# A four-layer transformer on one core: a new order of work inside the linear-attention stage

## The chip, the cores and the metric

The kernel runs on one core of a Trainium2 chip (trn2). The metric is the device time of one execution in microseconds (us), lower is better. A core has a matrix engine (TensorE, PE in the profile; PEld is its weight load), a vector engine (VectorE, DVE), an activation engine (ScalarE, ACT), a general engine (GpSimd, POOL) and a queue for transfers (SyncE, SP). Each engine works through its own list of instructions in order; semaphores hold an instruction back until another engine has done something. Matrix products go to PSUM, eight banks of 512 fp32 columns on 128 partitions.

## The reference

Four layers of cross-attention and feed-forward on x of 16 x 128 x 256, all in fp32. The change lies in the attention of the second layer, a linear attention, and in the routing of the mixture of experts behind it, which the kernel computes beside it:

```
x = x + _L1_xattn_ref(_layernorm(x), ctx, ctx, mask, Wq, bq, Wk, bk, Wv, bv, Wqf, Wkf, Wo, bo)
x = x + _L1_ffn_ref(_layernorm(x), wg_router, ...)

def _L1_xattn_ref(query, key, value, attention_mask, ...):     # 16 heads of 16, 64 features
    q, k, v = heads(query, Wq, bq), heads(key, Wk, bk), heads(value, Wv, bv)
    q_prime = relu(einsum('bhnd,fd->bhnf', q, Wqf))
    k_prime = relu(einsum('bhnd,fd->bhnf', k, Wkf)) * attention_mask
    kv = einsum('bhnf,bhne->bhfe', k_prime, v)
    qkv = einsum('bhmf,bhfe->bhme', q_prime, kv)
    qk_sum = einsum('bhmf,bhf->bhm', q_prime, sum(k_prime))
    return (qkv / (qk_sum + 1e-08)) @ Wo.T + bo

# _L1_ffn_ref, its head: scores = softmax(x2d @ wg_router.T); top 6 of 32 experts;
# the place of each token in its expert = running count over all tokens; rows are sent there
```

## The kernel before

The stage is `linear_attention` (L1161). It works on 16 rows of the batch (128 tokens each, i = 0 to 15) in four groups of four (t = 0 to 3; j is the row in its group; g = t - 1 is the group before). Its work stands written out by hand, one list for each engine; nothing schedules it.

**A group's head.** PE projects the group's queries (Q0, Q1, into the two banks `proj`) and keys (K0, K1, into the two banks `wide`) with 512 columns each, and computes the query features in four rounds R00, R10, R01, R11 (`query_features`, L1263): each fills two banks, which ACT empties with a ReLU into `qf` (`move_features`, L1399) before they are used again. Before, R00, R10 and R11 go to `proj` and R01 to `wide`. Between them PE mixes and sums up the last rows of the group before (`mix_up(i-1)`, `sum_up(i-2)`, `sum_up(i-1)`). K1 goes to the bank in which the row before lies mixed, so it waits for that row's normalisation.

**A row's slot (j).** `key_features` (L1283, into `proj`; ACT masks them, `mask`), `turn_row` (L1269: a transpose of a normalised row of the next group, ACT moves it, `move_row`), `mix_up(i-1)`, `sum_up(i-2)`, `values(i+1)` (L1276), `pair_up(i)` (L1295, keys by values into `wide[0]`, ACT moves it). The values and the turned row share one bank, `value`, in its two halves; a matmul to one half waits until DVE or ACT has read the other.

**DVE** adds the bias to the values (`move_values`, L1463), normalises the mixed row (`normalize`, L1469: a reciprocal and a product), adds the summed row to x (`update`, L1477), and does the routing of the group before: `variance`, `shifts`, `scale` in the head, `find_slots` of the group before that in slot 0, `soften` and `choose` (L1045, the top 8 of 32) in slot 2, `pick` (L1062, counts) in slot 3.

**POOL** takes the roots for the norms (`root`), adds a bias to rows of x, and sends the rows of finished groups to the experts with indirect transfers (`scatter`, L1110, six to a row, each row waiting until the row before has landed). Its list is: root 0, biases, root 1, then four rows sent with a bias behind each, root 2, three rows sent, root 3, root 4. A group's rows can be sent once `find_slots` for the group is done. The next stage (experts) begins when all engines have ended this one, and opens with the other nine rows' transfers on POOL.

Lines that the timelines name: L1260 projections, L1266 query features, L1273 row turn, L1280 values, L1292 key features, L1301 pairs, L1312 mix, L1320 sum, L1014 and L1030 routing on PE; L1466 values' bias, L1471 and L1474 normalise, L1481 and L1483 update, L999 and L1003 shift and scale, L1049 to L1060 choose, L1067 to L1070 pick, L1095 to L1107 find slots on DVE; L994 root and L1116 scatter on POOL; L1421 on ACT hands DVE the divisor `z` of a mixed row.

## Time and profile before

| | us |
|---|---|
| median of 3 runs | 2010.26 (2008.82 to 2015.07) |
| the profiled execution | 2015.13 |
| its span in the trace | 2013.4 |
| linear-attention stage in it | about 698 to 893 |
| PE busy over the span | 1792.1 (89%) |
| DVE / ACT / POOL busy | 1264.2 / 1026.1 / 729.0 |
| granted TensorE clock, mean | 0.963 |

The chain of waits that the profile prints ends in the last stage, which the change does not touch, so it says nothing of this one. What binds here is read from the timelines of the engines: in each, a row is one instruction or a run of like ones, with its start, its busy time, the instruction, and in brackets the idle time ahead of it and what ended that.

### The profile page before, as it was taken

The page shows a single profiled execution, that of the slowest core. Times are in us where ns is not written, and L with a number is a line of the kernel's source. Part 1 is how long each engine was busy: PE and PEld are TensorE (multiplying, and loading weights), DVE is VectorE, ACT ScalarE, POOL GpSimd, SP SyncE. Part 2 cuts the span into 40 slices and gives each one's busy share as a digit, 9 for nine tenths or more (in the row PEclk, how much of TensorE's full clock was granted, in tenths as well). Part 3 has the DMA queues.
Part 4 walks back from the last instruction along what each step waited for, and adds up shares of the span by engine and source line. Part 5 has one row for each costly group of instructions (what it writes and reads, how often), then busy time and mean ns, then how long its engine had stood idle before and what let it go on. Part 6 is the DMA issues. An engine that isn't in the chain of part 4 may idle for free. (4 is left out here: it accounts for less than half of the span.)

```text
span 2013.4 us, 42500 instructions
## 1 busy us (share of the span) xinstructions
PE 1792.1 (89%) x12207; PEld 1211.7 (60%) x12216; DVE 1264.2 (63%) x4137; ACT 1026.1 (51%) x2698; POOL 729.0 (36%) x707
## 2 busy tenths in 40 slices
PE   7999999998999888859899999987997879999765
PEld 4677777775555556645566666663554555787533
DVE  5666666664777534565543344446997954787697
ACT  5555555554333344411344444435887942666586
POOL 3333333332000100557455555552320011998420
PEclk9999999999999999979999999998998889999888
DMA  9990000000000000135577777650001021222100
GB/s 311 304 274 0 0 0 0 0 0 1 0 0 0 1 1 1 70 135 176 142 164 161 164 162 171 117 123 1 2 2 66 1 70 41 43 54 58 36 22 22
DMA packets 145607, 145.55 MB, mean 72 GB/s; under 512 B 49376, under 2 KB 133568, under 8 KB 145344
## 3 DMA queue, kind: packets, MB, share of 16 engines
q1 hardware_dynamic: 122432, 113.81, 19.5%
q0 software_dynamic: 23040, 30.01, 8.5%
q8 instruction: 75, 1.23, 0.3%
q14 instruction: 60, 0.49, 0.1%
HBM read 137.12 MB, written 66.44 MB: 101 GB/s over the span
## 5 line engine op out<-in xcount | busy, mean ns | idle before, releaser
L1709 POOL DMA_INDIRECT expert_sums<-moe_rows_in,moe_to x128 | 198.2, 1549 | 159.2 <-DMA expert_sums<-moe_rows_in,moe_to 101.6
L1782 PE MATMUL moe_gate<-moe_places,moe_xt 128*128 x512 | 175.9, 466 | 4.2 <-issue 2.0
L1975 DVE COPY moe_ht_e<-moe_turned 128x256 f32<-128x256 f32 x128 | 54.3, 424 | 194.4 <-PE moe_turned L1790 194.4
L570 ACT ACTIVATE ga_prob<-ga_score,ga_neg_max 128x128 f32<-128x128 f32 x256 | 99.6, 390 | 125.7 <-DVE ga_neg_max L443 125.7
L2065 POOL TENSOR_TENSOR ln_rstd<-ln_var,half 128x4 f32<-128x4 f32 (+1 forms) x16 | 21.4, 1338 | 367.2 <-DVE ln_var L2061 367.2
L190 POOL TENSOR_TENSOR ga_q_inv<-ga_q_sum,half 128x4 f32<-128x4 f32 x64 | 64.4, 1007 | 224.4 <-DVE ga_q_sum L426 224.4
L3325 DVE CUSTOM_DVE_ANT_0 ctxt<-wa_score,early 128x128 f32<-128x128 f32 x512 | 110.8, 287 | 46.9 <-PE wa_score L3171 46.9
L3141 POOL TENSOR_TENSOR ctxt<-ctxt,wa_top 128x512 f32<-128x512 f32 x128 | 129.8, 1040 | 17.1 <-DVE wa_top L3325 17.1
L325 PE MATMUL ga_summed<-ga_wo,ga_out_t 128*128 128x256 f32 x512 | 121.2, 380 | 0.7 <-ACT ga_out_t L578 0.7
L1782 PEld LDWEIGHTS moe_gate<-moe_places,moe_xt 128*128 128x128 f32 x512 | 90.8, 190 | 48.6 <-issue 13.6
L249 PE MATMUL ga_proj<-early,ga_xt 128*128 128x512 f32 x252 | 119.8, 598 | 0.0
L1116 POOL DMA_INDIRECT slot_x<-early x96 | 98.6, 1027 | 54.1 <-issue 27.1
L439 DVE SCALAR_TENSOR_TENSOR ga_score<-ga_scored,ga_q_inv,ga_mask 128x128 f32<-128x128 f32 x256 | 72.2, 344 | 51.6 <-PE ga_scored L297 51.2
L325 PEld LDWEIGHTS ga_summed<-ga_wo,ga_out_t 128*128 128x128 f32 x512 | 92.3, 190 | 11.0 <-ACT ga_out_t L578 1.1
L1889 ACT ACTIVATE moe_act_e<-moe_gate 128x176 f32<-128x176 f32 x128 | 40.6, 317 | 101.6 <-PE moe_gate L1782 101.6
L3180 PE MATMUL wa_turned<-ident,ctxt 128*128 128x128 f32 x512 | 77.3, 286 | 11.3 <-POOL ctxt L3141 10.0
L3274 ACT ACTIVATE wa_pt<-wa_turned 128x512 f32<-128x512 f32 x128 | 73.1, 596 | 25.8 <-PE wa_turned L3180 23.3
L431 DVE COPY ga_qt<-ga_turned 128x512 f32<-128x512 f32 x63 | 43.4, 689 | 62.6 <-PE ga_turned L289 62.5
L297 PEld LDWEIGHTS ga_scored<-ga_kt,ga_qt 128*128 128x128 f32 x512 | 63.7, 192 | 23.6 <-DVE ga_qt L431 13.9
L556 ACT ACTIVATE ga_square<-ga_q_tok 128x128 f32<-128x128 f32 x256 | 75.0, 294 | 1.5 <-DVE ga_q_tok L394 1.4
L297 PE MATMUL ga_scored<-ga_kt,ga_qt 128*128 128x128 f32 x512 | 72.5, 285 | 0.9 <-DVE ga_qt L431 0.9
L1884 ACT ACTIVATE moe_xt<-moe_up 128x256 f32<-128x256 f32 x128 | 49.2, 384 | 47.0 <-PE moe_up L1771 36.5
(491 smaller groups left out, 4700.2 us busy)
## 6 DMA issues: line engine op xcount, KB each, us to landing
moe_places<-in_L_ffn_packed SPq DMA_DIRECT2D x128, 608.0 KB
slot_x<-zeros SPq DMA_DIRECT2D x24, 1076.0 KB, 14.8
moe_rows_in<-slot_x SPq DMA_DIRECT2D x128, 134.5 KB, 3.2
wa_v<-v_ctx SPq DMA_DIRECT2D x16, 180.0 KB, 3.2
early<-in_L_xattn_Wq SPq DMA_DIRECT2D x5, 512.0 KB, 7.8
x<-in_x SPq DMA_DIRECT2D x4, 512.0 KB, 9.6
ga_wo<-in_L_xattn_Wo SPq DMA_DIRECT2D x1, 2048.0 KB, 15.0
expert_sums<-zeros SPq DMA_DIRECT2D x2, 1024.0 KB, 7.9
```

The lines of the kernel that those rows point to most:

```text
L249: last = pe.matmul(proj[m % 2][:, :], lhs[:, c, :], weight[:, c, :], start=(c == 0), stop=(c == HC - 1))
L297: last = pe.matmul(scored[n % 2][:, h * P:(h + 1) * P], qt[:, n % 2, h * P:(h + 1) * P], kt[:, b % 2, g, :], start=True, stop=True)
L325: last = pe.matmul(summed[:, 0:H], out_t[:, h, :], w.wo[:, h, :], start=(h == 0), stop=(h == NH - 1))
L556: last = act.activation(square[:, h, :], q_tok[:, n % 2, h * D:(h + 1) * D], ACT.Square, accum_out=q_sum[:, n % 2, h:h + 1])
L570: last = act.activation(prob[:, n % 2, part], score[:, n % 2, part], ACT.Exp, bias=neg_max[:, n % 2, h:h + 1], accum_out=total[:, n % 2, h ...
L1116: pool.indirect_dma_start(out=self.mem.slot_x, out_offset=bass.IndirectOffsetOnAxis(ap=self.slot_to[:, t, k:k + 1], axis=0), in_=self.mem. ...
L1709: pool.indirect_dma_start(out=mem.sums[j % SUMS], out_offset=bass.IndirectOffsetOnAxis(ap=to[:, j:j + 1], axis=0), in_=y[:, j, :], in_offs ...
L1782: last = pe.matmul(both[j % 2][:, 0:2 * FE], xt[:, j % 2, c, :], packed[:, place, c * 2 * FE:(c + 1) * 2 * FE].rearrange("p a n -> p (a n) ...
L3141: pool.tensor_tensor(unit, unit, top[:, k % LOWS, :].unsqueeze(2).to_broadcast([P, QUAD, P]), ALU.subtract).then_inc(lowered.sem, 1)
L3180: last = pe.transpose(turned[k % 2][:, x * P:(x + 1) * P], low[:, k % LOWS, x, :], mem.ident[:, :])
L3274: act.activation(pt[:, k // 2, :, k % 2, :], turned[k % 2][:, :].rearrange("p (x m) -> p x m", x=QUAD), ACT.Exp).then_inc(pt_moved.sem, 1)
L3325: ins = dve.tensor_tensor_reduce(unit[:, x, :], score[k % QUAD][:, x * P:(x + 1) * P], w.table[:, k, x, :], 1.0, NEVER, ALU.add, ALU.max, ...
```

## The change

Five edits, all of them of order, in three lists:

1. The features: R01 now goes to `proj` and R10 and R11 to `wide`; the round to `proj` comes first, and R11 stands behind the first row's key features, which wait for R01 alone.
2. In a slot, PE computes `values(i+1)` ahead of the mix, and the row turn comes last ahead of the pairs. `values` waits for the row move one earlier, and `turn_row(i)` for the bias addition of values i+1, not i.
3. ACT follows: R11's move behind the first mask, the divisor `z` ahead of the row move.
4. DVE at a group's border: `normalize(i-1)` ahead of `update(i-2)`; at the end, `normalize(15)` ahead of `variance(3)`.
5. DVE: `choose` in slot 3 behind that slot's update, just ahead of `pick`, not in slot 2.

```diff
-        Q0, Q1, K0, R00, K1, R10, R01, R11 = range(NP)
+        Q0, Q1, K0, R00, K1, R01, R10, R11 = range(NP)
...
                 def turn_row(i):
-                    pe.wait_ge(v_moved.sem, v_moved.at(i))
+                    pe.wait_ge(v_moved.sem, v_moved.at(i + 1))
...
                 def values(i):
-                    behind(pe, row_moved, min(i, B - GROUP) - 1)
+                    behind(pe, row_moved, min(i - 1, B - GROUP) - 1)
...
                     if j == 0:
-                        pe.wait_ge(moved.sem, moved.at(t * NP + R11))
+                        pe.wait_ge(moved.sem, moved.at(t * NP + R01))
...
-                    query_features(t, R10, proj, 1, 0)
+                    query_features(t, R01, proj, 0, 1)
                     pe.wait_ge(moved.sem, moved.at(at + K1))
-                    query_features(t, R01, wide, 0, 1)
-                    pe.wait_ge(moved.sem, moved.at(at + R10))
-                    query_features(t, R11, proj, 1, 1)
+                    query_features(t, R10, wide, 1, 0)
...
     # DVE, at a group's border
+                        normalize(i - 1)
                         update(i - 2)
-                        normalize(i - 1)
                         update(i - 1)
...
     # DVE, slots 2 and 3
                             router.soften(dve, g)
+                        if g >= 0 and j == 3:
                             router.choose(dve, g)
-                        if g >= 0 and j == 3:
                             router.pick(dve, g)
                 update(B - 2)
+                normalize(B - 1)
                 dve.wait_ge(counted.sem, counted.at(B - 3))
                 router.variance(dve, G - 1)
-                normalize(B - 1)
```

PE, the last features of a group's head and its first slot, before (the second group, in which routing work of the first stands too; the semaphores in brackets are those that an instruction waits for):

```order
L1266 MATMUL la_proj<-la_qt,la_fq 128x512 [waits la_moved]
L1266 MATMUL la_wide<-la_qt,la_fq 128x512 [waits la_moved]
L1266 MATMUL la_proj<-la_qt,la_fq 128x512 [waits la_moved]
L1292 MATMUL la_proj<-la_fk,la_kt 128x256 [waits la_moved]
L1273 MATMUL la_value<-ident,la_xn 128x128 [waits la_v_moved,la_row_normed]
L1280 MATMUL la_value<-la_wv,ctxt 128x256 [waits la_row_moved,la_v_moved]
L1301 MATMUL la_wide<-la_v,la_kf 128x64 [waits la_v_moved,la_kv_moved,la_masked,la_moved]
L1014 MATMUL la_route<-ident,early 128x128 [waits mr_scaled]
```

The same place in the changed kernel:

```order
L1266 MATMUL la_proj<-la_qt,la_fq 128x512 [waits la_moved]
L1266 MATMUL la_wide<-la_qt,la_fq 128x512 [waits la_moved]
L1292 MATMUL la_proj<-la_fk,la_kt 128x256 [waits la_moved]
L1266 MATMUL la_wide<-la_qt,la_fq 128x512 [waits la_moved]
L1280 MATMUL la_value<-la_wv,ctxt 128x256 [waits la_row_moved,la_v_moved]
L1273 MATMUL la_value<-ident,la_xn 128x128 [waits la_v_moved,la_row_normed]
L1301 MATMUL la_wide<-la_v,la_kf 128x64 [waits la_v_moved,la_kv_moved,la_masked,la_moved]
L1014 MATMUL la_route<-ident,early 128x128 [waits mr_scaled]
```

The key features (L1292) moved ahead of the last query features, and the values (L1280) ahead of the row turn (L1273).

DVE from the end of the second group to the head of the third, before (`early` holds the router's small tiles):

```order
L1049 TENSOR_REDUCE early<-early 128x4
L1060 CAST early<-early 128x4x6
L1466 TENSOR_TENSOR la_v<-la_value,la_bv 128x8x32
L1471 RECIPROCAL la_z_inv<-la_z 128x256
L1481 TENSOR_TENSOR x<-x,la_out 128x256
L1067 TENSOR_TENSOR early<-early 128x768
L1070 TENSOR_TENSOR early<-early 128x32 x4
L1481 TENSOR_TENSOR x<-x,la_out 128x256
L1471 RECIPROCAL la_z_inv<-la_z 128x256
L1481 TENSOR_TENSOR x<-x,la_out 128x256
```

And in the changed kernel, whose lines there are numbered two higher:

```order
L1468 TENSOR_TENSOR la_v<-la_value,la_bv 128x8x32
L1473 RECIPROCAL la_z_inv<-la_z 128x256
L1483 TENSOR_TENSOR x<-x,la_out 128x256
L1049 TENSOR_REDUCE early<-early 128x4
L1060 CAST early<-early 128x4x6
L1067 TENSOR_TENSOR early<-early 128x768
L1070 TENSOR_TENSOR early<-early 128x32 x4
L1473 RECIPROCAL la_z_inv<-la_z 128x256
L1483 TENSOR_TENSOR x<-x,la_out 128x256
L1483 TENSOR_TENSOR x<-x,la_out 128x256
```

The choice (L1049 to L1060) moved behind the slot's normalisation and update and stands in a row with the pick; the border's normalisation moved ahead of the first of the two updates. (Some rows between are left out in both.)

## Rows read from the trace of the kernel before

**Rows 1.** Busy time by stretch: PE, PEld, DVE, ACT, POOL, granted clock, DMA share, GB/s
```profile
734.90:781.20 46.30, 40.65 (x323) 27.57 (x322) 18.64 (x50) 21.24 (x36) 3.90 (x5) 0.96 0.00 1
781.20:825.80 44.60, 39.02 (x325) 26.97 (x323) 24.58 (x66) 19.96 (x35) 13.99 (x15) 1.00 0.10 35
872.00:893.50 21.50, 6.10 (x52) 4.70 (x50) 13.58 (x45) 1.24 (x3) 7.82 (x10) 0.59 0.12 43
```

**Rows 2.** Timeline of PE, third group: start, busy, line, instruction, idle ahead
```profile
791.86 1.98 PE L1260 MATMUL la_wide<-ctxt,la_wk 128*128 128x512 f32 x4 [2.09 <-DVE la_mixed_t L1474]
...
794.64 1.13 PE L1266 MATMUL la_proj<-la_qt,la_fq 64*128 64x512 f32 x4
...
796.89 1.13 PE L1266 MATMUL la_proj<-la_qt,la_fq 64*128 64x512 f32 x4 [0.27 <-ACT la_qf L1401]
799.14 1.14 PE L1292 MATMUL la_proj<-la_fk,la_kt 64*128 64x256 f32 x8 [1.12 <-ACT la_qf L1401]
...
801.86 1.10 PE L1280 MATMUL la_value<-la_wv,ctxt 128*128 128x256 f32 x4 [1.21 <-ACT xnt L1392]
802.79 1.89 PE L1301 MATMUL la_wide<-la_v,la_kf 128*128 128x64 f32 x16
...
807.77 1.10 PE L1280 MATMUL la_value<-la_wv,ctxt 128*128 128x256 f32 x4 [0.20 <-ACT xnt L1392]
...
823.10 1.10 PE L1280 MATMUL la_value<-la_wv,ctxt 128*128 128x256 f32 x4 [0.69 <-ACT xnt L1392]
```

**Rows 3.** Timeline of POOL: roots (L994) and the ends of two chains of scatters
```profile
808.12 1.23 POOL L1116 DMA_INDIRECT slot_x<-early  x1 [10.51 <-DVE early L1107]
...
846.27 1.07 POOL L994 TENSOR_TENSOR early<-early,half 128x4 f32<-128x4 f32 x1
853.72 1.04 POOL L1116 DMA_INDIRECT slot_x<-early  x1 [6.39 <-DVE early L1107]
...
881.23 0.74 POOL L994 TENSOR_TENSOR early<-early,half 128x2 f32<-128x2 f32 x1
```

**Rows 4.** Timelines of DVE (two rows) and PE (one) in the fourth group
```profile
847.37 0.16 DVE L999 SCALAR_TENSOR_TENSOR early<-early 128x4 f32<-128x4 f32 x1 [6.20 <-POOL early L994]
...
882.08 0.15 DVE L999 SCALAR_TENSOR_TENSOR early<-early 128x2 f32<-128x2 f32 x1
...
849.95 0.63 PE L1014 MATMUL la_route<-ident,early 128*128 128x128 f32 x4 [1.84 <-DVE early L1096]
```

**Rows 5.** Timeline of PE at the second group's border, and busy time by stretch
```profile
745.56 3.21 PE L1260 MATMUL la_wide<-ctxt,la_wk 128*128 128x512 f32 x4 [2.17 <-DVE la_mixed_t L1474]
...
750.03 1.13 PE L1266 MATMUL la_proj<-la_qt,la_fq 64*128 64x512 f32 x4
...
746.00:748.00 2.00, 2.00 (x4) 0.88 (x3) 0.00 (x0) 0.00 (x0) 0.00 (x0) 0.54 0.00 0
```

**Rows 6.** Timeline of DVE: choose, pick, normalise, and a later bias addition
```profile
776.97 0.29 DVE L1049 TENSOR_REDUCE early<-early 128x4 f32<-128x128 f32 x1 [0.37 <-ACT early L1043]
...
779.11 0.18 DVE L1060 CAST early<-early 128x24 f32<-128x24 uint32 x1
...
783.05 0.94 DVE L1067 TENSOR_TENSOR early<-early 128x768 bf16<-128x768 f32 x1
...
785.55 0.81 DVE L1070 TENSOR_TENSOR early<-early 128x32 bf16<-128x32 bf16 x4
...
789.54 1.74 DVE L1471 RECIPROCAL la_z_inv<-la_z 128x256 f32<-128x256 f32 x1
791.38 0.42 DVE L1474 TENSOR_TENSOR la_mixed_t<-la_wide,la_z_inv 128x256 f32<-128x256 f32 x1
...
803.06 0.42 DVE L1466 TENSOR_TENSOR la_v<-la_value,la_bv 128x256 f32<-128x256 f32 x1 [3.83 <-PE la_value L1280]
```

**Rows 7.** Who waited for whom, 698 to 893 us: total, times, longest
```profile
DVE la_v L1466 <- PE la_value L1280: 59.3, 14, 14.9
```

**Rows 8.** Timelines of ACT and DVE, last row's divisor and its normalisation
```profile
867.04 0.38 ACT L1421 ACTIVATE la_z<-la_wide 128x256 f32<-128x256 f32 x1
...
868.39 1.75 DVE L1471 RECIPROCAL la_z_inv<-la_z 128x256 f32<-128x256 f32 x1
...
866.04 0.29 DVE L1049 TENSOR_REDUCE early<-early 128x4 f32<-128x128 f32 x1 [0.38 <-ACT early L1043]
```

More of the change, by code:

```diff
@@ L1346, in _ @@
                     pe.wait_ge(moved.sem, moved.at(at + R00))
-                    query_features(t, R10, proj, 1, 0)
+                    query_features(t, R01, proj, 0, 1)
                     pe.wait_ge(moved.sem, moved.at(at + K1))
-                    query_features(t, R01, wide, 0, 1)
-                    pe.wait_ge(moved.sem, moved.at(at + R10))
-                    query_features(t, R11, proj, 1, 1)
+                    query_features(t, R10, wide, 1, 0)
                     for j in range(TG):
                         key_features(i + j)
-                        if t < G - 1:
-                            turn_row(i + j)
+                        if j == 0:
+                            pe.wait_ge(moved.sem, moved.at(at + R10))
+                            query_features(t, R11, wide, 1, 1)
+                        if i + j + 1 < B:
+                            values(i + j + 1)
                         if j >= 1:
@@ L1359, in _ @@
                             sum_up(i + j - 2)
-                        if i + j + 1 < B:
-                            values(i + j + 1)
+                        if t < G - 1:
+                            turn_row(i + j)
                         if j == 0:
-                            pe.wait_ge(moved.sem, moved.at(at + R01))
+                            pe.wait_ge(moved.sem, moved.at(at + R11))
                         if g >= 0 and j == 1:
@@ L1435, in _ @@
                     move_projection(t, K1, kt, wide[:, 1, :], w.bk, 1)
-                    move_features(t, R10, proj, 1, 0)
-                    move_features(t, R01, wide, 0, 1)
-                    move_features(t, R11, proj, 1, 1)
+                    move_features(t, R01, proj, 0, 1)
+                    move_features(t, R10, wide, 1, 0)
                     for j in range(TG):
                         mask(i + j)
+                        if j == 0:
+                            move_features(t, R11, wide, 1, 1)
+                        if j >= 1:
+                            move_mixed(i + j - 1)
                         if t < G - 1:
@@ L1444, in _ @@
                                 norm_row(i + j + 1)
-                        if j >= 1:
-                            move_mixed(i + j - 1)
                         if g >= 0 and j == 1:
```

## The prediction

> **What bounds the stage now.** I read the stretches of the linear-attention stage first. PE is busy for 40.65 of 46.30 us in the second group and 39.02 of 44.60 in the third, POOL for 3.90 and 13.99 [rows 1]. So in the first three groups PE sets the pace, and what is there to be had is its idle time. The timeline of PE in the third group shows where that is: 2.09 us ahead of K1, which waits for the normalisation; 0.27 and 1.12 ahead of the last query features and of the key features, which wait for ReLUs; 1.21, 0.20 and 0.69 ahead of the values of three of its rows, which wait for a row move [rows 2]. That is 5.58 us in a group of 44.6. The first group has the same without the border's wait and without the 0.20 and 0.69, the second group all of it.
>
> Next POOL. It starts to send rows at 808.12, as soon as the slots of the first group are known, and is then a chain of its own: four rows and four biases, and root 2 from 846.27, 39.22 us after the first transfer has started, end included. DVE stands idle 6.20 us for that root, and PE 1.84 us behind DVE [rows 3, 4]. From DVE's L999 at 847.37 it takes 6.35 us until POOL sends again (853.72), and three rows and root 3 later it is 881.97; DVE's next L999 is at 882.08 [rows 3, 4]. So **from the third group's first slot on, POOL sets the end of the stage**, with DVE 0.1 us behind it. What PE gains after that slot is hidden under POOL. What it gains before moves POOL's start, and the whole rest with it. The question is therefore: how much earlier is the first group's find_slots, that is, DVE's bias addition at 803.06 [rows 6]? The stages behind start when this one ends, and nothing else is in flight (DMA share 0.00 in the second group [rows 1]), so I take their lengths as they are.
>
> **The change part by part, up to that addition.** All starts are of this trace; g is the gain so far.
>
> *Features on other banks.* A round of features in `proj` and back takes 796.89 - 794.64 = 2.25 us, and the next 799.14 - 796.89 = 2.25: PE 1.13, ACT's ReLU, the way there and back [rows 2]. Before, the key features wait for two such rounds behind K1's sum, now for one, with R10 in `wide` beside it: 2.25 saved at each head. In the first group the key features move from 711.8 to 709.6 by the same rule (2.25).
>
> *Values first.* Behind the key features, before: from 799.14 to the pairs at 802.79 is 3.65, with the 1.21 in it [rows 2]. Now: key features 1.07 (1.14 less the overlap of starts), R11 0.98 (moved here, no longer saved), values until DVE has added the bias, 1.10 + 0.10 + 0.42 + 0.06 = 1.68, and the turn 0.37: 4.10. **The new wait** of turn_row on the addition costs about 0.75 us here, since nothing stands between values and turn in slot 0, and with R11 it makes the slot 0.45 longer. Queued behind the turn are the pairs, and behind them ACT's move. In slots 1 to 3 the mix (1.0) or mix and sum (2.0) stand between, so the addition is done by then: DVE waits for the values and not they for it, 59.3 us in 14 waits [rows 7]. There 0.20 goes in slot 1 and 0.69 in slot 3 (with the restart, 0.22 and 0.86), and in the first group's slot 1 0.32.
>
> *Border.* Before, the normalisation ends at 791.80 and K1 starts at 791.86 after 2.09 us idle [rows 2, 6]. Without the update ahead of it, it starts when z is there: at the second group's border nothing else is on DVE, and the whole 2.17 goes (2.23 with the restart).
>
> *Choice later.* The choice takes 779.29 - 776.97 = 2.32 us, the pick 786.36 - 783.05 = 3.31, and normalisation 2.26 [rows 6]. Before, the choice lay in slot 2, under PE work, though it held back the next addition. Now choice and pick stand in a row ahead of the border's normalisation. At the third group's border I get: z of row 6 at 770.35, normalise and update until 773.40, choice until 775.72, pick until 779.03, normalised at 781.30, K1 at 781.36. PE is ready for K1 at 780.75. So 0.6 of the 2.09 stays as a wait and 1.6 is gained with what goes at the restart. Had the choice stayed, the addition of row 8 would wait for the exponent, and the turn behind it.
>
> *Clock.* At the second border the granted clock is 0.54, the 1.2 GHz level, after 2.17 us without a matmul: K1 takes 3.21 against 1.98, and from K1 to the next features it is 4.47 us against 2.78 at the third border [rows 2, 5]. Without that wait I count those 1.69 as saved.
>
> **The sum.** First group: head 2.25, slot 0 -0.45, slot 1 0.32, rest 0: g = 2.1. Second: border 2.23, clock 1.69, features 2.25, slot 0 -0.45, slot 1 0.22, slot 3 0.86: g = 8.9. Third: border 1.6, features 2.25: 12.75 at the key features. The values then come after key features and R11, with the 1.21 and the turn (0.37) no longer ahead of them, 2.05 after the key features against 2.72 before: g = 13.4. DVE's scaling, ahead of the addition, ends 0.9 earlier than the values, so it does not hold them. POOL's first transfer moves from 808.12 to 794.7, root 2 and all behind it too.
>
> *Fourth group and end.* PE and DVE run ahead and wait for POOL. From 849.95 - 13.4 on the order of PE is nearly that of before. But DVE: before, the choice starts at 866.04 and from there DVE is busy without a gap until L999 at 882.08; z of row 14 is there at 867.42 [rows 4, 8]. Now normalise comes first and needs that z. Values first lets the normalisation of row 13, the update, softening, exponent and mask come 1.0 earlier, so z is there at 866.4; DVE then has 2.26 + 0.8 + 2.32 + 3.31 + 0.8 + 2.26 + 0.7 + 3.6 = 16.0 us of the same work, so L999 is at 882.4, 0.35 later than by POOL. The variance moved behind normalise(15) (879) is still ahead of POOL's free time (881.2), no cost. Gain at the end: 13.4 - 0.35 = 13.05. If nothing came 1.0 earlier it would be 12.05; if POOL alone bound, 13.4.
>
> *The pause.* PE, now ahead, stands still in the fourth group not for 1.84 us [rows 4] but for about 4.8. Rows bound what that does to the clock: after 2.09 us the level stayed at 2.4 GHz [rows 2], after 2.17 it was 1.2 [rows 5], and in the end of the stage, where PE is busy 6.10 of 21.50 us, it is 0.59 on average [rows 1]. Bounds: 0 and 1.7 us (the 1.69 above, for like work), perhaps 2.2. PE's work behind the pause leads to that last choice on DVE, so a loss there counts in full. I take 1.7: 4.8 is more than twice the wait that cost it. The Trainium skill (TensorE: Matmul & The Clock Gate, What's actually happening) says "the default state is throttled, and activity releases the throttle"; rows 5 agree (0.54 after a wait), and by it the pause costs the 1.7, where by the 2.09 us row it would cost nothing and the time would be 1.7 lower.
>
> So 13.05 - 1.7 = 11.35 us. The profiled execution was 2015.13, 4.87 above the median; the gain taken from it gives 2003.8, and from the median 2010.26 it gives **1998.9**.
>
> **The rivals.**
> *The clock at its best.* No low stretch in the fourth group: gain 13.05, 1997.2. For it: three of the waits of about 2 us left the clock alone. Chance 0.15.
> *The turn waits in every slot.* If DVE's addition is late in slots 1 to 3 too, because DVE is busy, six more turns ahead of POOL's start cost 0.75 to 1.2 each: 4.5 to 7.2, gain 4.2 to 6.9, 2003.4 to 2006.1. For it: in the second group's slot 0 DVE's scaling ends only 0.1 us ahead of the values, and slot 3 has more on DVE now. Against it: DVE's idle time [rows 7]. Chance 0.15, half of it on each side of 0.3%.
> *The dip of the clock was chance.* If other runs lack it, or another wait brings it back elsewhere, the 1.69 isn't gained: 2000.6. It lies in the forecast's range, with it 0.62.
> *Hidden.* The gain reaches POOL but is given back in the experts' stage (its transfers then find another phase of weights and clock): up to 11 given back, 1999 to 2010. Nothing in rows speaks for it. Chance 0.04.
> *Slower.* The mechanism is the clock: if the pause of 4.8 us in the fourth group or the turn's waits let the level fall to 1.2 GHz and keep it there, each us of full-speed work costs another. To end 6 us above 2010.26 it must cost 17.4 us more than the forecast, nearly half of a group's 40 us of PE work [rows 1] at the low level. Before, the low stretch was over 4.5 us after it began [rows 5] and the group's mean is 0.96. A whole group at 1.2 GHz would give 2038. Chance 0.04.
> *It doesn't do what it says* (PE waits at K1 and the features as before, since something else held them): 2010. The releasers in rows 2 name the very instructions that move. It is in the chance of "same".
>
> **How the numbers follow.** Forecast with its clock variants 0.62 + 0.15, turn 0.15, hidden 0.04, slower 0.04. Range: the low end is the best clock less 2 for the spread of medians, 1995.0; the high end takes in the lost clock gain, the 1.0 of the tail and most of the turn rival, 2005.0. A measurement here can tell about 0.3%, 6 us, from no change, so faster means below 2004.2: 0.62 + 0.15 + 0.07 + 0.02 = 0.86; slower 0.04; same 0.10.
>
> **What the profile after would show.** Right: key features of the first group 2.2 us sooner; K1 of the second group without a wait, at full clock, that of the third with 0.6; a wait of about 0.75 ahead of the turn in slot 0 only, released by the values' addition; the first scatter near 795, root 2 near 833, the next start of scatters near 840; a pause of PE of 4 to 5 us in the fourth group; the stage ending 11 to 13 us sooner. Wrong: waits ahead of turns in slots 1 to 3, first scatter later than 800, or POOL idle between the root and its next rows for longer than 6.4 us. The forecast falls too if the stages behind are not as long as before.

## The result, and the profile after

| | before | after |
|---|---|---|
| median, us (runs) | 2009.65 (6) | 2000.59 (6) |
| lowest to highest | 2006.95 to 2015.07 | 1996.45 to 2004.56 |
| profiled execution / its span | 2015.13 / 2013.4 | 1996.45 / 1994.7 |

The ratio is 0.9949 (95%: 0.9927 to 0.9971): faster by 0.5%. The forecast was 1998.9. The changed kernel was measured a second time on another chip: 2003.45 against 2015.32, ratio 0.9935 (0.991 to 0.9959). For that run a ratio of 0.9935 to 0.9965 had been expected, a first scatter again 96.3 us into the stage if no stretch of low clock falls ahead of it, and the low clock again behind the pause of the fourth group; all three came (96.33 us, and key features of 2.08 us behind a pause of 5.00).

The profiled spans differ by 18.7 us, and only part of that is the change's. I count from the stage's first matmul (`values(0)`) to the next stage's first matmul: 195.37 us before, 184.60 after, 10.77 less. The other 8 us lie ahead of the stage (698.17 against 694.55) and behind it (1119.9 against 1115.6), in code that is the same. In the fourteen traces of this study the stage starts anywhere between 692.4 and 698.8, whatever the edit. So everything below is told **from the stage's own first matmul**, and compared piece by piece.

The groups of the stage after, columns as in rows 1:

```profile
694.55:729.20 34.65, 33.77 (x261) 22.37 (x261) 10.73 (x21) 17.95 (x29) 8.99 (x18) 1.00 0.01 2
729.20:768.66 39.46, 38.51 (x323) 26.49 (x322) 16.62 (x33) 21.65 (x36) 3.91 (x5) 1.00 0.01 1
768.66:808.62 39.96, 38.70 (x325) 26.69 (x324) 25.13 (x67) 20.49 (x35) 14.14 (x15) 1.00 0.11 39
808.62:858.00 49.38, 41.22 (x348) 28.06 (x347) 28.34 (x84) 18.18 (x30) 28.66 (x30) 0.93 0.21 74
```

The second group takes 39.46 us where it took 46.30, the third 39.96 where it took 44.60 [rows 1], and PE is idle in them for 0.95 and 1.26 us. The granted clock is 1.00 in the first three groups. What is left of the waits, on PE in the third group:

```profile
777.59 1.98 PE L1260 MATMUL la_wide<-ctxt,la_wk 128*128 128x512 f32 x4 [0.32 <-DVE la_mixed_t L1476]
...
780.36 1.13 PE L1266 MATMUL la_proj<-la_qt,la_fq 64*128 64x512 f32 x4
781.33 1.02 PE L1266 MATMUL la_wide<-la_qt,la_fq 64*128 64x512 f32 x4
782.62 1.13 PE L1292 MATMUL la_proj<-la_fk,la_kt 64*128 64x256 f32 x8 [0.27 <-ACT la_qf L1402]
783.58 1.08 PE L1266 MATMUL la_wide<-la_qt,la_fq 64*128 64x512 f32 x4
784.59 1.13 PE L1280 MATMUL la_value<-la_wv,ctxt 128*128 128x256 f32 x4
786.40 0.41 PE L1273 MATMUL la_value<-ident,la_xn 128*128 128x128 f32 x2 [0.68 <-DVE la_v L1468]
786.64 1.96 PE L1301 MATMUL la_wide<-la_v,la_kf 128*128 128x64 f32 x16
```

Against rows 2: the wait for the normalisation went from 2.09 to 0.32. The two waits of 0.27 and 1.12 ahead of the last query features and the key features have become one of 0.27. The values wait for no row move, and the new wait of the turn for the values' bias is 0.68. That wait stands in slot 0 of each of the first three groups (0.61, 0.68, 0.68) and in no other slot. K1 of the second group, 3.21 us after a wait of 2.17 in rows 5, now waits for nothing:

```profile
737.62 1.98 PE L1260 MATMUL la_wide<-ctxt,la_wk 128*128 128x512 f32 x4
```

POOL starts to send 96.33 us into the stage (before 109.95) and, as rows 3 of before, is a chain from there. The end, on POOL, DVE and PE:

```profile
790.88 1.23 POOL L1116 DMA_INDIRECT slot_x<-early  x1 [7.54 <-DVE early L1107]
...
829.11 1.07 POOL L994 TENSOR_TENSOR early<-early,half 128x4 f32<-128x4 f32 x1
...
836.56 1.04 POOL L1116 DMA_INDIRECT slot_x<-early  x1 [6.39 <-DVE early L1107]
...
864.16 0.72 POOL L994 TENSOR_TENSOR early<-early,half 128x2 f32<-128x2 f32 x1 [0.28 <-DVE early L989]
...
830.20 0.16 DVE L999 SCALAR_TENSOR_TENSOR early<-early 128x4 f32<-128x4 f32 x1 [8.00 <-POOL early L994]
...
867.63 0.15 DVE L999 SCALAR_TENSOR_TENSOR early<-early 128x2 f32<-128x2 f32 x1
```

Before, DVE's L999 for root 3 came 0.1 us behind that root [rows 3, 4]. Now root 3 ends at 864.88 and DVE uses it at 867.63, so DVE is the last of the two, by 2.75 us. (Root 4 and its L999 follow 6.4 us after that L999 in every trace.) DVE's delay begins with a pause of PE:

```profile
832.78 1.09 PE L1014 MATMUL la_route<-ident,early 128*128 128x128 f32 x4 [5.17 <-DVE early L1096]
833.80 2.08 PE L1292 MATMUL la_proj<-la_fk,la_kt 64*128 64x256 f32 x8
835.81 1.72 PE L1280 MATMUL la_value<-la_wv,ctxt 128*128 128x256 f32 x4
837.47 1.08 PE L1312 MATMUL la_wide<-la_qf,la_kv 128*32 128x128 f32 x32
...
829.00:837.00 8.00, 4.21 (x15) 2.91 (x16) 5.27 (x16) 1.67 (x2) 1.61 (x3) 0.58 0.06 19
```

PE is idle for 5.17 us, as DVE stands 8.00 us for the root. Behind the pause the key features take 2.08 us, where they take 1.13 at full clock; the granted clock of the stretch is 0.58.

### The profile page after: what moved, and what is told of

It reads as the page before. It is cut to its first block and busy times, and to the rows that moved or that the text cites. A ratio compares the mean times of both kernels' runs of the same rounds, so it can differ in the third digit from the quotient of the medians.

```text
span 1994.7 us, 42500 instructions
## 1 busy us (share of the span) xinstructions
PE 1789.1 (90%) x12207; PEld 1210.3 (61%) x12216; DVE 1261.6 (63%) x4137; ACT 1028.1 (52%) x2698; POOL 729.2 (37%) x707
```

## The experiments

The kernels before and after and the twelve further runs in one table, in us from the stage's first matmul, from one trace of each. "L999 of root 3" is the instruction with which DVE uses root 3. "Low clock" lists the stretches in which the granted clock is 0.50, the 1.2 GHz level, that begin in the first 155 us (later PE's work thins out, and the clock is low somewhere in all of them). The ratio is the whole kernel's time to the kernel before on the same chip, with its 95% interval. These intervals are 4 to 9 us either way, so small differences between two kernels are read from the stage, not from the ratio.

| kernel | first scatter | L999 of root 3 | next stage | low clock | ratio |
|---|---|---|---|---|---|
| before | 109.95 | 183.91 | 195.37 | 48-51 | |
| after | 96.33 | 173.08 | 184.60 | 136-142 | 0.9949 (0.9927-0.9971) |
| after, again | 96.33 | 173.48 | 184.85 | 137-144 | 0.9935 (0.991-0.9959) |
| border alone | 108.33 | 183.21 | 194.58 | 55-65, 113-116, 150-154 | 0.9985 (0.9961-1.0009) |
| features alone | 107.51 | 184.39 | 195.85 | 46-50, 91-94, 149-156 | 0.9973 (0.9947-0.9999) |
| values alone | 109.03 | 183.63 | 195.15 | 48-51, 69-72, 150-154 | 0.9972 (0.9952-0.9991) |
| choice back | 99.01 | 173.33 | 184.85 | 75-79, 137-144 | 0.9943 (0.9918-0.9969) |
| last group alone | 112.75 | 188.50 | 200.01 | 16-27, 153-160 | 1.0007 (0.9984-1.003) |
| root ahead | 96.32 | 168.29 | 179.82 | none | 0.9928 (0.9899-0.9957) |
| filler | 96.31 | 170.82 | 182.29 | none | 0.9923 (0.9897-0.9949) |
| root, choice back in last group | 97.91 | 169.74 | 181.27 | 62-65 | 0.9907 (0.9882-0.9933) |
| root, three rows in flight | 96.32 | 165.83 | 177.34 | none | 0.9917 (0.9885-0.995) |
| root, three rows, choice back in last group | 96.33 | 164.27 | 175.80 | 154-157 | 0.9895 (0.9851-0.994) |
| root ahead, on before | 116.75 | 193.53 | 204.90 | 48-52, 58-69, 99-103, 110-120 | 1.0002 (0.9968-1.0035) |

### Each part alone

**The border alone**, on the kernel before:

```diff
-                        update(i - 2)
                         normalize(i - 1)
+                        update(i - 2)
                         update(i - 1)
```

> The kernel before with edit 4 alone at the borders (normalise ahead of the two updates). Read in the trace, from the stage's first matmul: before, the first scatter starts at 110.0 us and DVE's last L999 of the fourth group at 183.9. My theory: PE is the limit until the first group's slots are found, so each border's wait counts in full: 2.2 at the second group, 2.1 at the third, and 1.7 more if the low clock behind the first of them goes. First scatter at 104.0 (105.7 without the clock), end of the stage sooner by about as much, at most 2 us less because PE's pause in the fourth group grows to about 4 us. Rival (another engine holds K1 anyway): first scatter within 0.5 of 110.0.

Measured: 108.33, not 104.0. From the second group's Q0 to its key features it takes 15.71 us against 19.65, 3.94 saved (2.23 and 1.69 were counted for that), and in the third 15.83 against 17.98, 2.15 saved. Then from key features to the next Q0 of the second group, where the edit touches nothing on PE's path, it takes 31.09 against 26.62: 4.47 lost. 3.94 + 2.15 - 4.47 = 1.62, the whole difference. Where the 4.47 went, on PE and by stretch:

```profile
748.22 1.14 PE L1292 MATMUL la_proj<-la_fk,la_kt 64*128 64x256 f32 x8 [1.12 <-ACT la_qf L1401]
749.29 0.44 PE L1273 MATMUL la_value<-ident,la_xn 128*128 128x128 f32 x2
750.94 2.05 PE L1280 MATMUL la_value<-la_wv,ctxt 128*128 128x256 f32 x4 [1.21 <-ACT xnt L1392]
752.78 3.52 PE L1301 MATMUL la_wide<-la_v,la_kf 128*128 128x64 f32 x16
...
757.08 2.08 PE L1292 MATMUL la_proj<-la_fk,la_kt 64*128 64x256 f32 x8
...
751.00:753.00 2.00, 2.00 (x6) 1.64 (x7) 0.00 (x0) 0.28 (x1) 0.72 (x1) 0.50 0.00 0
```

Behind the two waits of slot 0, 1.12 and 1.21, the values take 2.05 us for 1.10 and the pairs 3.52 for 1.89 [rows 2], and the clock stays at 1.2 GHz from 55 to 65 us, although PE is busy. The same two waits in the kernel before left the clock at full speed in rows 2. Without the 4.47 the first scatter would be at 103.86, the 104.0 of the theory; the whole kernel's ratio doesn't tell this part from no gain.

**The features alone**, on the kernel before:

```diff
-        Q0, Q1, K0, R00, K1, R10, R01, R11 = range(NP)
+        Q0, Q1, K0, R00, K1, R01, R10, R11 = range(NP)
...
-                        pe.wait_ge(moved.sem, moved.at(t * NP + R11))
+                        pe.wait_ge(moved.sem, moved.at(t * NP + R01))
...
                         key_features(i + j)
+                        if j == 0:
+                            pe.wait_ge(moved.sem, moved.at(at + R10))
+                            query_features(t, R11, wide, 1, 1)
```

> The kernel before with the query features on other banks alone (R01 to proj, R10 and R11 to wide, R11 behind the first key features, with ACT's moves). My theory: the key features start one round of features (2.25 us) sooner in each group, R11 then costs 0.98 in the slot, since the row move behind it still holds the values: 1.27 net in each of three groups, first scatter at 106.1 us from the stage's first matmul against 110.0 before. Rival: ACT, now with the mask and R11 in a row, holds the row turn and values longer, and the net is 0.5 or less a group: 108.5 or later.

Measured: 107.51, which is neither the theory's 106.1 nor the rival's 108.5. The key features of the first group come 2.25 sooner (11.41 against 13.66 us), its end 1.34 sooner. The second group's head is 2.26 shorter and the rest of it 0.93 longer (R11 lies there now). The third head gains only 0.69, as the clock is low at 91 to 94. The fourth head gains 2.25 again (15.73 against 17.98). So the part is worth what was counted, and the low stretch took 1.6 of it: 107.51 - 1.6 = 105.9.

**The values alone**, on the kernel before:

```diff
-                    pe.wait_ge(v_moved.sem, v_moved.at(i))
+                    pe.wait_ge(v_moved.sem, v_moved.at(i + 1))
...
-                    behind(pe, row_moved, min(i, B - GROUP) - 1)
+                    behind(pe, row_moved, min(i - 1, B - GROUP) - 1)
...
                         key_features(i + j)
-                        if t < G - 1:
-                            turn_row(i + j)
+                        if i + j + 1 < B:
+                            values(i + j + 1)
```

(with the turn at the place where the values were, and ACT's `move_mixed` ahead of `move_row`.)

> The kernel before with the values ahead of mix and row turn alone (and z ahead of the row move on ACT); features, border and choice as before. My theory: the waits of 1.21, 0.20 and 0.69 for the row move go, about 0.75 for the addition comes in slot 0 only; in slot 3 the choice in slot 2 holds the addition of the next row, so that the 0.7 to 0.9 there turn into a loss of about 1. First scatter at 107.5 us (106 if the choice does not hold it) against 110.0. Rival (the turn waits in every slot): waits of 0.75 or more ahead of L1273 in slots 1 to 3 as well, first scatter at 110 or later.

Measured: 109.03, where 107.5 was expected. The first group gains 0.74, and in the third the first scatter comes 1.62 sooner behind the key features (7.36 against 8.98). In the second group the slots take 28.12 against 26.62: 1.50 lost, with a low stretch at 69 to 72 and a turn wait of 1.20 in slot 3, where the choice (still in slot 2) held back DVE's addition. With 0.06 at the second head that makes the 0.92. The third group's slots as a whole take 25.44 against 26.63 us, with turn waits of 0.68 in slot 0 and 0.16 in slot 3. The new wait of slot 0, on PE in the first group:

```profile
715.26 0.41 PE L1273 MATMUL la_value<-ident,la_xn 128*128 128x128 f32 x2 [0.61 <-DVE la_v L1466]
```

**The choice back in slot 2**, on the changed kernel:

```diff
                             router.soften(dve, g)
-                        if g >= 0 and j == 3:
                             router.choose(dve, g)
+                        if g >= 0 and j == 3:
                             router.pick(dve, g)
```

> The changed kernel with edit 5 undone: the choice is back in slot 2. My theory: in slot 3 of the second group the addition of row 8 stands behind exponent and choice, the turn of row 7 waits about 1.6 us for it, and the wait at the third border (0.3) goes: first scatter at 97.6 us from the stage's first matmul against 96.3 with the change. At the end DVE has the choice done while it waits for z, which gives back 0.7: last L999 of the fourth group at 173.6 against 173.1. Rival (choice and pick in a row at the border cost more than they save): first scatter at 95.7 or sooner.

Measured: 99.01 for 96.33, where 97.6 was expected. The second group's slots take 27.49 against 26.01 us: 1.48 lost, and this is where:

```profile
769.24 0.29 DVE L1049 TENSOR_REDUCE early<-early 128x4 f32<-128x128 f32 x1 [1.40 <-ACT early L1043]
...
771.60 0.42 DVE L1468 TENSOR_TENSOR la_v<-la_value,la_bv 128x256 f32<-128x256 f32 x1
...
772.17 0.41 PE L1273 MATMUL la_value<-ident,la_xn 128*128 128x128 f32 x2 [1.19 <-DVE la_v L1468]
...
774.26 5.23 PE L1260 MATMUL la_proj<-xnt,la_wq 128*128 128x512 f32 x8
```

DVE stands 1.40 us for the exponent, then chooses, and the addition that the turn needs comes 1.19 too late for PE. Behind that wait the next projections run at the low clock (granted 0.50 over 774 to 776), which costs the third head another 1.19 net: 1.48 + 1.19 = 2.67 of the 2.68. But the fourth group has the choice early too, and there it is a gain of 2.43 where 0.7 was expected: from the first scatter to the L999 of root 3 it takes 74.32 us against 76.75. Of the 2.43, 1.77 lie between the L999 of root 2 and that of root 3 (35.66 against 37.43), where DVE makes the choice while it would stand for z. So moving the choice later gains 2.7 at the front and gives 2.4 back at the end. The two kernels reach the next stage at 184.85 and 184.60, and their ratios are alike: over the whole stage edit 5 in all groups brought nothing that this run can tell.

### What sets the end

**The new order in the last group alone**, on the kernel before: features, values and border as in the change, but for `t == G - 1` only.

```diff
+                NEW = (G - 1,)
...
+                        pe.wait_ge(moved.sem, moved.at(t * NP + (R01 if t in NEW else R11)))
...
+                        if t in NEW and i + j + 1 < B:
+                            values(i + j + 1)
```

> The kernel before with the new order (features, values, border) in the fourth group alone; the choice stays in slot 2. My theory: the fourth group is held by POOL's chain of scatters and root, so nothing is gained: first scatter at 110.0 us from the stage's first matmul as before, the last L999 of the fourth group at 183.9, or up to 2.0 later if PE's pause, grown from 1.84 to about 5 us, brings the clock to its low level. Rival (PE sets the pace of this group too): 3 to 5 us sooner.

Measured: nothing gained, 1.0007 (0.9984 to 1.003). PE's key features of the fourth group come 4.41 us sooner behind Q0 (13.57 against 17.98), but POOL's root 3 comes only 0.72 sooner behind the first scatter (73.13 against 73.85). From the first scatter to the L999 of root 3 it takes 75.75 us against 73.96 before, within the 2.0 that was allowed for the low clock (it is low at 153 to 160). PE gets ahead and stands the longer:

```profile
850.63 1.09 PE L1014 MATMUL la_route<-ident,early 128*128 128x128 f32 x4 [5.41 <-DVE early L1096]
```

This shows that what PE gains behind the first scatter is hidden under POOL, all but 0.7 us. The first scatter itself, 112.75, was later than 109.95 in code that this edit doesn't change. Its first group has a low stretch of 10 us, again behind the waits of slot 0:

```profile
712.37 2.05 PE L1282 MATMUL la_value<-la_wv,ctxt 128*128 128x256 f32 x4 [1.21 <-ACT xnt L1404]
...
715.00:717.00 2.00, 2.00 (x11) 2.00 (x11) 0.00 (x0) 0.00 (x0) 0.00 (x0) 0.50 0.00 0
```

It costs 4.49 us (the second Q0 at 41.21 against 36.72); the dip at the second border is missing in this execution, 1.69 us the other way (44.58 against 46.27 for the second group): 4.49 - 1.69 = 2.80, the whole difference.

**Root 2 ahead of the fourth row**, on the changed kernel, so that it lies in the wait for a transfer to land and DVE gets it a row sooner:

```diff
                 for t in range(GROUP):
+                    if t == GROUP - 1:
+                        router.root(pool, 2)
                     router.scatter(pool, t)
                     bias(3 * GROUP + t)
-                router.root(pool, 2)
```

> The changed kernel with root 2 on POOL ahead of the fourth row's transfers, not behind its bias. My theory: DVE and PE of the fourth group wait for that root and for nothing else, so PE's pause (5.17 us) goes, and with it the low clock behind it (2.0), and POOL sends its rows 4 to 6 without waiting for DVE: last L999 of the fourth group at 166 to 168 us from the stage's first matmul against 173.1, the time about 6 us less than the changed kernel's. Rival (the chain of scatters alone sets the end, whatever the root): 172 or later, no change of the time.

Measured: L999 of root 3 at 168.29, 4.8 sooner; the expectation was 166 to 168. PE has no pause there, the clock isn't low until 157, and POOL sets the end again:

```profile
826.48 1.04 POOL L994 TENSOR_TENSOR early<-early,half 128x4 f32<-128x4 f32 x1 [2.77 <-DVE early L989]
...
847.81 0.97 POOL L1116 DMA_INDIRECT slot_x<-early  x1 [2.37 <-DMA slot_x<-early]
...
866.32 0.75 POOL L994 TENSOR_TENSOR early<-early,half 128x2 f32<-128x2 f32 x1
...
831.87 0.61 PE L1014 MATMUL la_route<-ident,early 128*128 128x128 f32 x4
...
867.10 0.16 DVE L999 SCALAR_TENSOR_TENSOR early<-early 128x2 f32<-128x2 f32 x1 [2.33 <-POOL early L994]
```

L1014 takes 0.61 for 1.09, and DVE now waits 2.33 for root 3. The 6 us expected of the whole kernel can't be told: its interval, 0.9899 to 0.9957, overlaps those of the changed kernel.

**Filler in the pause**, on the changed kernel: eight matmuls whose result nobody uses, in the bank's free half, just ahead of the wait. They are extra work.

```diff
+                        if t == G - 1 and j == 0:
+                            pe.wait_ge(added.sem, added.at(i - 1))
+                            for n in range(4):
+                                for c in range(HC):
+                                    pe.matmul(out[:, H:2 * H], mem.ctxt[:, c, i * P:(i + 1) * P], w.wv[:, c, :], start=(c == 0), stop=(c == HC - 1))
```

> The changed kernel with eight matmuls of 256 columns put in PE's pause of the fourth group, into a half bank that nobody reads (they compute nothing that is used). My theory: the pause costs 2.0 us through the clock. Filled for 4 of its 5 us, the clock stays at its high level, L1014 behind it takes 0.6 and not 1.09, and the last L999 of the fourth group is 2.0 sooner, at 171.1 against 173.1. Rival (the 2.7 us that DVE ends behind POOL are all from its own new order): 173.1 with or without.

Measured: the wait is 1.48, and all behind it runs at full clock.

```profile
827.75 3.67 PE L1372 MATMUL la_out<-la_wv,ctxt 128*128 128x256 f32 x16
...
832.90 0.63 PE L1014 MATMUL la_route<-ident,early 128*128 128x128 f32 x4 [1.48 <-DVE early L1096]
833.46 1.13 PE L1292 MATMUL la_proj<-la_fk,la_kt 64*128 64x256 f32 x8
...
865.73 0.15 DVE L999 SCALAR_TENSOR_TENSOR early<-early 128x2 f32<-128x2 f32 x1
```

The L999 of root 3 comes 170.82 us into the stage, 2.26 sooner than in the changed kernel, though PE does more. Of the 2.26, 0.24 lie ahead of the pause's end: root 2 comes that much sooner into the stage in this execution (its L999 at 135.41 against 135.65). From the L999 of root 2 to that of root 3 it is 35.41 against 37.43. **This shows the price of the low clock by itself: 2.0 us**, and that the pause caused it: the clock fell in the pause of 5.17, and in those of 5.00 (changed kernel again) and 4.32 (choice back), and stayed up where the pause was filled. In the second trace of the changed kernel the same stretch took 37.92, so another execution can pay 2.5.

**The root ahead and the choice back, in the last group only:**

```diff
-                        if g >= 0 and j == 3:
+                        if g >= 0 and j == (2 if t == G - 1 else 3):
                             router.choose(dve, g)
```

> The changed kernel with root 2 ahead of the fourth row's transfers, and the choice of the last of the three full groups back in slot 2. My theory: DVE waited 1.79 us for z of row 14 with the choice still to do; in slot 2 it fits in there. With the root ahead, last L999 of the fourth group at 165.5 to 167.5 us from the stage's first matmul, about 0.7 sooner than with the root alone. Rival: the normalisation of row 14 then comes later and holds the sum of row 14: no difference to the root alone, or 0.5 later.

Measured: from the first scatter to the L999 of root 3 it takes 71.83 us, and 71.97 without this edit. That is nothing, as the rival had it, since POOL sets that end; the 0.7 expected didn't come. Its first scatter is 1.6 later by a low stretch at 62 to 65, in code of the changed kernel that kept the full clock in the other traces, and with no wait ahead of it:

```profile
752.30 1.90 PE L1302 MATMUL la_wide<-la_v,la_kf 128*128 128x64 f32 x16
754.03 1.99 PE L1030 MATMUL la_scores<-early,xnt 128*128 128x32 f32 x16
755.95 2.08 PE L1293 MATMUL la_proj<-la_fk,la_kt 64*128 64x256 f32 x8
757.96 1.71 PE L1281 MATMUL la_value<-la_wv,ctxt 128*128 128x256 f32 x4
...
756.00:759.00 3.00, 3.00 (x12) 2.00 (x12) 0.00 (x0) 0.92 (x1) 0.00 (x0) 0.50 0.00 0
```

The last wait of PE ahead of it is the 0.68 of slot 0, 10 us earlier. The values' run (69 to 72) and the border's run (113 to 116) have such a stretch too, and in all three it begins right behind L1030, sixteen matmuls of 32 columns. At the 25 other places of L1030 in the second and third groups of the fourteen traces the clock stays up. Its ratio, 0.9907, is inside the interval of the root alone.

**Three rows in flight**, on the kernel with the root ahead. A row's six transfers waited until the row before had landed; now they wait for the row three ahead, whose semaphore they share.

```diff
-        if 1 <= t <= EARLY_ROWS:
-            pool.wait_ge(self.mem.scattered[(t - 1) % SCATTERS].sem, 16 * TOPK * ((t - 1) // SCATTERS + 1))
+        if SCATTERS <= t <= EARLY_ROWS:
+            pool.wait_ge(self.mem.scattered[t % SCATTERS].sem, 16 * TOPK * (t // SCATTERS))
```

> The changed kernel with root 2 ahead of the fourth row's transfers and, beside that, each row sent to the experts waiting for the landing of the row three before, not of the row before. My theory: with the root ahead POOL's chain set the end by 2.33 us; without five waits of 1.6 to 2.4 us it no longer does, and DVE sets it: last L999 of the fourth group at 166.0 us from the stage's first matmul against 168.3 with the root alone and 173.1 with the change. Rival (rows in flight together land slower and hold POOL or the next stage): 168 or later.

> The same as e11 with the choice of the last full group back in slot 2. With the root alone that choice gave nothing, as my theory has it because POOL set the end; now that DVE sets it, it should give the 0.7 us: last L999 at 165.3 against 166.0. Rival (the choice costs elsewhere what it saves): 166.0 or later.

Measured: 165.83 without and 164.27 with the choice back in slot 2 of the last group. 166.0 and 165.3 had been expected. The landing waits are gone, and now DVE's variance is what POOL stands for:

```profile
822.21 1.04 POOL L994 TENSOR_TENSOR early<-early,half 128x4 f32<-128x4 f32 x1 [5.33 <-DVE early L989]
...
832.31 0.99 POOL L1116 DMA_INDIRECT slot_x<-early  x1 [0.17 <-issue]
...
857.10 0.72 POOL L994 TENSOR_TENSOR early<-early,half 128x2 f32<-128x2 f32 x1 [1.50 <-DVE early L989]
...
860.57 0.15 DVE L999 SCALAR_TENSOR_TENSOR early<-early 128x2 f32<-128x2 f32 x1
```

With DVE as the bound the choice counts, and with 1.56 us for more than the 0.7 expected, where it had counted for nothing under POOL. The last kernel reaches the next stage 175.80 us in, 8.80 sooner than the change and 19.6 sooner than before, at 1993.57 us, ratio 0.9895 (0.9851 to 0.994). That is the fastest median of the study (the changed kernel had 2003.45 on the same chip), though the intervals of several of these kernels overlap.

**The root ahead, on the kernel before** (the same edit as above):

> The kernel before with root 2 ahead of the fourth row's transfers alone. My theory: there PE's pause is only 1.84 us and POOL starts its last rows only 1.5 sooner, so it is worth little by itself: last L999 of the fourth group 74.0 - 1.6 = 72.4 us behind the first scatter, where the same edit on top of the change gives 72.0 against 76.8 (4.8 sooner). Rival (the edit is worth as much either way): 4 to 5 us sooner, 69 to 70 behind the first scatter.

Measured: 116.75 and 193.53, both later than before, and neither number of the expectation. Four low stretches lie in the first 120 us, and the edit seems to cost something itself in this execution:

```profile
849.49 1.04 POOL L994 TENSOR_TENSOR early<-early,half 128x4 f32<-128x4 f32 x1 [7.06 <-DVE early L989]
```

The root needs DVE's variance, which comes late as PE is late, and now the fourth row of transfers stands behind it for 7.06 us; root 2 no longer has a whole row's time as cover. From the first scatter to the L999 of root 3 it takes 76.78 us, against 73.96 before. How much of the 2.8 lost is the low clock and how much the edit's, this run doesn't tell.

## Why the prediction was right, and where it wasn't

**The sum up to the first scatter**, piece by piece, at full clock in both kernels but for the dip that was counted as saved:

| piece | before, us | after, us | gained | predicted |
|---|---|---|---|---|
| first group | 36.72 | 34.65 | 2.07 | 2.1 |
| second, Q0 to key features | 19.65 | 13.45 | 6.20 | 2.23 + 1.69 + 2.25 = 6.17 |
| second, its slots | 26.62 | 26.01 | 0.61 | 0.63 |
| third, Q0 to key features | 17.98 | 13.96 | 4.02 | 1.6 + 2.25 = 3.85 |
| third, to first scatter | 8.98 | 8.26 | 0.72 | 0.65 |
| sum | | | 13.62 | 13.4 |

Each term held, the new wait of the turn too (0.61 to 0.68, counted as 0.75). The wait left at the third border is 0.32 and not 0.6. One reading was wrong without harm: the first group is said to lack the 0.20 of slot 1, but the trace of before has it there (at 720.02), and the sum counts its 0.32. That an early choice holds back the addition was right as a mechanism: 1.48 is lost at once with the choice back, and with the low stretch behind it 2.68, where 1.3 net was expected. That the choice is therefore better in slot 3 is not borne out, since the end gives 2.43 of it back.

**That POOL's start sets the end** was right: the features, values and border edits in the last group alone gave nothing, and the 13.62 at the first scatter arrived as 13.47 at POOL's root 3 (183.80 against 170.33).

**The end on DVE.** The loss from the first scatter to the L999 of root 3 is 2.79 us (76.75 against 73.96) where 2.05 was predicted. Its two terms are told apart by the filler. The low clock cost 2.02, not 1.7; the rest is 0.77, of which 0.70 is the order of DVE (normalise ahead, waiting for z, choice and pick behind it; 35.41 against 34.71 from one L999 to the next), not 0.35. That 0.70 is a net: the late choice by itself costs 1.56 to 1.77 (the last two kernels with three rows in flight, and the choice back), so PE's new order must give about 1 us of it back, which the prediction had also counted; no run shows that 1 us alone. The wait for z is there:

```profile
851.62 1.75 DVE L1473 RECIPROCAL la_z_inv<-la_z 128x256 f32<-128x256 f32 x1 [1.79 <-ACT la_z L1422]
```

The clock term was mis-sized because it was taken from one dip of one K1. After the pause, turn, key features and values take 4.69 us (832.78 to 837.47) against 2.68 in the filler's run (832.90 to 835.58): those 2.01 are the whole price, and it reaches DVE's L999 in full, as the prediction said. The pause itself is 5.17, predicted about 4.8. The variance behind normalise(15) holds root 3 back by 0.28, where no cost was counted; since DVE's L999 comes 2.75 later than the root, it costs nothing.

**The number.** Gained at the L999 of root 3: 10.83, predicted 11.35. 2010.26 less 11.35 gave 1998.9; the medians differ by 9.06, and the interval (5.8 to 14.7 us, from 0.9927 to 0.9971) holds both. It is too wide to confirm single terms; those rest on the pieces of the traces above. That the forecast came within 1.7 us of the median is in part luck, since single executions of one kernel lie 8 us apart. Two signs were missed narrowly: the stage ends 10.77 us sooner and not 11 to 13, and the pause is 5.17 and not 4 to 5.

**The step that failed, though the number stood**, is that single stretches of low clock are a matter of the border. I took the 1.69 of one execution as a property of its place, and called the rival "the dip was chance". The runs show something in between, and larger. Of the five traces with the old border (before, features, values, last group, root on before) four have a dip at the second border and one hasn't. At the third border, after 2.08 or 2.09 us, two of the five have one. In slot 0, behind 0.27, 1.12 and 1.21 us of waits, the clock stayed up in rows 2; of the twelve such places in the first three groups of four traces (before, border, last group, root on before) four are followed by a low stretch of 10 us, at 4.2 to 4.5 where the whole of it could be read. All six kernels with old waits show one to four low stretches that begin ahead of their first scatter. Of the eight with all the new orders of PE, six had none there and reached the first scatter at 96.31 to 96.33; the two others had one of 3 to 4 us each, one behind the 1.19 us wait of its own edit and one behind no wait at all. That is also why the parts alone add up to 1.62 + 2.44 + 0.92 = 4.98 us at the first scatter and together make 13.62. Of the 8.64 between them, 4.47 and 1.6 are low stretches in the runs of the border and the features, and 2.11 lie in the second group's slots of the values' run (1.50 lost, where the change gained 0.61), by the choice's hold on the addition and a low stretch. A part of the gain of the change may be that it takes away what such stretches begin with. How large that part is on average over executions, the traces (one for each run) can't say. That the waits start such stretches is argued from their place, and shown only for the pause of 5.17 us, which the filler took away. What starts the three with no wait right ahead, all behind L1030 (62 to 65, 69 to 72 and 113 to 116 above), stays open; the same unknown cause may have a part in the others.

**The rivals.** Turn waits in every slot: this one fell, there is none in slots 1 to 3. The clock at its best: it fell, since the key features behind the pause take 2.08 us in both traces of the change. The dip was chance: half right, as said. Hidden: the part behind the stage is 4.3 us shorter, not longer, and among the twelve further runs it lies anywhere between 1112.0 and 1122.6 us, so the 4.3 can't be put down to the change. Slower by the clock: it fell; the low stretch was over within 7 us.

## What to carry to other kernels

Where two engines hand work to and fro, find the last instruction that another queue's chain starts from (here the first scatter), and count gains only up to there; behind it, the same three orders gave a ratio of 1.0007 (0.9984 to 1.003). Compare traces from landmark to landmark and piece by piece: 8 of the 18.7 us between two spans lay in unchanged code, and five pieces that each held to 0.2 us said more than the medians. A long pause of PE that an edit makes can be filled or taken away by what it waits for: bringing POOL's root forward one row gave 4.8 us of the stage, and letting three rows of transfers fly 2.5 more, against the 10.8 of the whole change.

## What the runs showed of the hardware

**The clock falls after short waits too, and not each time.** Behind 1.12 and 1.21 us of waits, with only a row's turn and key features between them, the granted clock went to 0.50 for about 10 us of busy PE at four places of twelve, and stayed at full speed at the others with the same instructions and waits. One such stretch cost 4.2 to 4.5 us, the short ones 1.2 to 1.7 (1.69 at the border, 1.6 at 62 to 65), the one after a 5.17 us pause 2.0. The Trainium skill (TensorE: Matmul & The Clock Gate, What's actually happening) says that activity releases the throttle. The traces agree in that the clock came back during busy work each time, but it took 10 us of busy matmuls at four places, behind waits of little more than 1 us. For a comparison of two orders it means that one trace of each can mislead by over 4 us at any place with such waits.

**Transfers of several rows in flight don't delay POOL's issue.** With each row waiting for the one before, POOL stood 1.5 to 2.4 us for each row's landing; with three rows in flight most issues still follow each other at 1.28 us, without such a wait (0.17 in its place), and the stage ends 2.5 us sooner.
